# Three stages of an eight-stage transformer kernel: attention with dense experts in two parts over all 32 batches, ReLU experts and a ternary feed-forward without their loops

## The reference, cut to what matters

```python
# stage E (L1_ffn): 16 heads of 8, 8 experts, 2 chosen for each row
q, k, v = split(x @ W_qkv + b_qkv)
attn_out = softmax(q @ k.T / sqrt(8)) @ v
gate = softmax(x @ W_gate + b_gate);  combine = gate kept at its two largest
out = attn_out + sum_e combine[e] * (x @ W_experts[e] + b_experts[e])
# stage G (L2_ffn): 8 experts 128 -> 512 -> 128, mask = 1 at the two largest gates
out = sum_e mask[e] * (relu(x @ w1[e] + b1[e]) @ w2[e] + b2[e])
# stage I (L3_ffn): weights rounded to -1, 0, 1
h = layernorm(gelu(x @ W_fc.T), w, b);  out = h @ W_proj.T
```

## Time and profile before

| what | value |
|---|---|
| median of 3 timed runs | 8145.55 us (8137.73 to 8151.84) |
| profiled execution | 8119.01 us, its span 8117.1 us |
| busy PE / PE weight loads / DVE / ACT / POOL | 79% / 59% / 62% / 35% / 10% |
| mean granted PE clock | 0.829 |

### The profile page before, as it was taken

How to read it: one execution, slowest core, us unless ns; L and a number is a source line. 1 busy time by engine, 2 the same in 40 slices (tenths; PEclk the granted TensorE clock), 3 DMA queues, 4 the chain that set the end, 5 groups by cost and what they waited for, 6 DMA issues and landing times. The chain is left out here.

```text
span 8117.1 us, 210088 instructions
## 1 busy us (share of the span) xinstructions
PE 6394.4 (79%) x89378; PEld 4794.1 (59%) x89401; DVE 5039.5 (62%) x17947; ACT 2829.9 (35%) x4816; POOL 831.3 (10%) x803
## 2 busy tenths in 40 slices
PE   4444589989866698988978868888888888888875
PEld 3333467766643388888856645556556555565653
DVE  6777855455456666666643367577575775756742
ACT  2121133333322311111111135555455554555541
POOL 1114400000000100000000011111110111101100
PEclk7667799999988855555579989999999999999986
DMA  1000000000000000000000000000000000000000
GB/s 31 1 2 1 27 1 1 1 1 1 1 4 0 3 4 4 4 4 4 4 22 0 0 18 2 7 6 2 10 2 4 8 2 10 2 2 10 2 4 10
DMA packets 61243, 45.06 MB, mean 6 GB/s; under 512 B 22521, under 2 KB 56125, under 8 KB 60227
## 3 DMA queue, kind: packets, MB, share of 16 engines
q1 hardware_dynamic: 60355, 32.26, 1.5%
HBM read 30.14 MB, written 2.10 MB: 4 GB/s over the span
## 5 line engine op out<-in xcount | busy, mean ns | idle before, releaser
L368 DVE TENSOR_REDUCE peak<-ps 128x8 f32<-128x1024 f32 (+1 forms) x832 | 816.8, 1023 | 267.1 <-PE ps L290 266.3
L410 ACT ACTIVATE e<-ps,H_lowT_c 77x1024 f32<-77x1024 f32 x384 | 405.6, 1105 | 259.9 <-PE ps L314 259.9
L410 ACT ACTIVATE e<-ps,H_lowT_s 128x1024 f32<-128x1024 f32 x384 | 407.0, 1111 | 248.5 <-PE ps L314 248.5
L328 PEld LDWEIGHTS ps<-e,H_vt 128*32 128x32 f32 (+1 forms) x12288 | 319.8, 112 | 255.5 <-ACT e L410 140.9
L328 PE MATMUL ps<-e,H_vt 128*32 128x128 f32 (+1 forms) x12288 | 432.9, 281 | 23.6 <-DVE xs L388 17.7
L314 PE MATMUL ps<-H_qr,H_km 32*128 32x128 f32 (+1 forms) x12288 | 424.6, 277 | 0.0
L314 PEld LDWEIGHTS ps<-H_qr,H_km 32*128 32x128 f32 (+1 forms) x12288 | 410.2, 170 | 15.4 <-issue 2.2
L1838 PE MATMUL ps<-F_hp,F_encW 128*128 128x1 bf16 (+2 forms) x12288 | 363.4, 166 | 24.7 <-issue 22.4
L1868 PE MATMUL ps<-F_eT,F_ctxp 77*128 77x1 f16 (+1 forms) x12288 | 375.4, 165 | 1.7
L418 ACT ACTIVATE oT<-ps 128x512 f32<-128x512 f32 x416 | 248.4, 597 | 365.9 <-PE ps L328 365.9
L2216 POOL TENSOR_TENSOR H_rstd<-H_veps,neghalf 128x4 f32<-128x4 f32 (+1 forms) x146 | 160.8, 1101 | 2076.3 <-DVE H_veps L2212 2076.3
(11 more groups left out here) (602 smaller groups left out, 14394.4 us busy)
## 6 DMA issues: line engine op xcount, KB each, us to landing
G_w<-in_L_ffn_w SPq DMA_DIRECT2D x16, 256.0 KB
H_f<-in_L_xcond_f_w SPq DMA_DIRECT2D x12, 256.0 KB
H_nw<-in_L_xcond_n_w SPq DMA_DIRECT2D x21, 128.0 KB, 2.1
A_cond<-in_cond SPq DMA_DIRECT2D x1, 2048.0 KB
out_x<-x_all SPq DMA_DIRECT2D x1, 2048.0 KB, 8.7
ctx_rows<-in_ctx SPq DMA_DIRECT2D x1, 1232.0 KB
D_wq<-in_L_xcond_attn_wq SPq DMA_DIRECT2D x2, 512.0 KB
D_wk<-in_L_xcond_attn_wk SPq DMA_DIRECT2D x2, 512.0 KB
```

Source lines behind the costliest of these rows:

```text
L328: last = nc.tensor.matmul(ps[PAD_COLS * s:PAD_COLS * (s + 1), FLAT, r * S:(r + 1) * S], vt_of(u)[0:keys, QUAD * r + s, :], e[0:keys, half, ...
L368: last = nc.vector.tensor_reduce(peak[:, HL * half:HL * (half + 1)], view, AX.X, ALU.max, negate=True)
L410: nc.scalar.activation(e[0:keys, half, :], ps[0:keys, AGAIN[half]:AGAIN[half] + 2, :].rearrange("p b t -> p (b t)"), ACT.Exp, bias=low(u) ...
```

## The change

All three hardware loops are gone; the eight groups are written out in one block each, with counting semaphores in place of the barrier.

In **E** the work is split. The first part takes projections, gates and experts for all 8 groups; queries, keys and value rows of all 32 batches are kept (`qr`, `kr`, `vr`). An expert is now one job over the 4 batches of a group, in one of 4 banks, and DVE adds it at once into `x_all` with 4 scalar-tensor-tensor instructions; the wide multiply, the sum over experts and the tile `moe` are gone. The next group's transposes, projections and logits stand between jobs, at places that `TURN_AT` to `PICK_AT` name. The second part is one attention of 32 units, with the key masks made by ACT within it, values spread by POOL, and the sum into `x_all` after every fourth unit. The statistics of all 32 batches are taken in the preparation. In **G** and **I** the next group's layer norm, transposes and gates move between the experts (G) or beside the hidden layer (I) of the present one; the first group's statistics move to the preparation.

```diff
-km = sb("E_km", [D, QUAD, U * S], scope=st)
-o8 = sb("E_o8", [S, U, D], scope=st)
-moe = sb("E_moe", [S, U, D], scope=st)
+nT = sb("E_nT", [D, 2, U * S], scope=st)
+qr = sb("E_qr", [D, B * S], scope=st)
+kr = sb("E_kr", [D, B * S], scope=st)
+vr = sb("E_vr", [S, B, D], scope=st)
+km = sb("E_km", [D, 2, QUAD, U * S], scope=st)
...
-with nc.Fori(0, NG) as g:
-    with nc.Block() as block:
+with nc.Block() as block:
+    LOGITS, QUERY, KEY, VALUE = 4, 5, 6, 7
+    TURN_AT, QUERY_AT, KEY_AT, VALUE_AT, GATE_AT = 0, 1, 2, 3, 4
+    NORMAL_AT, CENTRE_AT, PICK_AT = 4, 6, 7
+    JOBS = NG * EXPERTS
...
+        def turn(g):
+            pe.wait_ge(sem["z_ready"], g + 1)
+            if g:
+                pe.wait_ge(sem["cand_ready"], g)
+            for u in range(U):
+                last = nc.tensor.transpose(ps[:, LOGITS, u * S:(u + 1) * S], zn[:, u, 0:D], ident[:])
+            last.then_inc(sem["zT_done"], 1)
...
+        turn(0)
+        query(0)
+        logits(0)
+        key(0)
+        value(0)
+        for g in range(NG):
+            for x in range(EXPERTS):
+                j = EXPERTS * g + x
+                if j >= 4:
+                    pe.wait_ge(sem["expert_ready"], j - 3)
+                lay_bias(per(j % 4), for_each(be[:, x * D:(x + 1) * D]))
+                for u in range(U):
+                    last = nc.tensor.matmul(per(j % 4)[:, u, :], nT[:, g % 2, u * S:(u + 1) * S], we[:, x * D:(x + 1) * D], start=False,
+                                            stop=(u == U - 1), skip_group_check=True)
                 last.then_inc(sem["expert_done"], 1)
...
+                if g + 1 < NG:
+                    if x == TURN_AT:
+                        turn(g + 1)
+                    if x == QUERY_AT:
+                        query(g + 1)
+                    if x == KEY_AT:
+                        key(g + 1)
+                    if x == VALUE_AT:
+                        value(g + 1)
+                    if x == GATE_AT:
+                        logits(g + 1)
...
+        def ready(u):
+            g = u // U
+            if u == 0:
+                pe.wait_ge(sem["expert_ready"], JOBS)
...
+                pe.wait_ge(sem["masked_v"], 2)
+            if u % U == 0:
+                pe.wait_ge(sem["masked_a"], QUAD * g + 2)
...
+        small_tensor(pe, 0, B, S, lambda u: qr[:, u * S:(u + 1) * S],
+                     lambda u: km[:, (u // U) % 2, :, (u % U) * S:(u % U + 1) * S],
+                     lambda u: vt[:, (u // U) % 2, u % U], None, ready, ready_values)
...
+        def during(u, part):
+            if part == 1 and u % U < 2 and u + U < B:
+                mask(u // U + 1, 2 * (u % U))
+                mask(u // U + 1, 2 * (u % U) + 1)
+        take(0)
+        take_query(0)
+        gate_exponentials(0)
+        take_key(0)
+        take_rows(0)
+        for g in range(1, NG):
+            take(g)
+            take_query(g)
+            take_key(g)
+            take_rows(g)
+            gate_exponentials(g)
+            if g == 2:
+                mask(0, 2)
+                mask(0, 3)
+        small_scalar(act, 0, B, S, None, during)
...
+        def during(u):
+            if u % U == 2 and u > U:
+                g = u // U - 1
+                dve.wait_ge(sem["o_normed"], U * g + U)
+                xg = x_all[:, g * U:(g + 1) * U, :]
+                step(nc.vector.tensor_tensor(xg, xg, o8[:], ALU.add))
+        normalise(0)
+        normalise(1)
+        centre_gates(0)
+        pick(0)
+        for g in range(NG):
+            for x in range(EXPERTS):
+                j = EXPERTS * g + x
+                dve.wait_ge(sem["expert_done"], j + 1)
+                for u in range(U):
+                    row = x_all[:, g * U + u, :]
+                    last = nc.vector.scalar_tensor_tensor(out=row, in0=per(j % 4)[:, u, :], scalar=picked[:, g % 2, u, x:x + 1],
+                                                          in1=row, op0=ALU.mult, op1=ALU.add)
+                last.then_inc(sem["expert_ready"], 1)
+                dve.wait_ge(sem["expert_ready"], j + 1)
+                if x == NORMAL_AT and g + 2 < NG:
+                    normalise(g + 2)
+                if x == CENTRE_AT and g + 1 < NG:
+                    centre_gates(g + 1)
+                if x == PICK_AT and g + 1 < NG:
+                    pick(g + 1)
+                if x == NORMAL_AT and g + 1 == NG:
+                    mask_first()
+        small_vector(dve, step, 0, B, S, lambda u: o8[:, u % U, :], during)
+        dve.wait_ge(sem["o_normed"], B)
...
+    TURN_AT, GATE_AT, PICK_AT = 4, 5, 6
+    pairs = [(g, x) for g in range(NG) for x in range(EXPERTS)]
...
+        turn_rows(pe, 0, bank=TURN)
+        logits(0)
+        hidden(0)
+        for m, (g, x) in enumerate(pairs):
+            if x == TURN_AT and g + 1 < NG:
+                pe.wait_ge(sem["gate_ready"], g + 1)
+                turn_rows(pe, g + 1, bank=TURN)
+            if m + 1 < len(pairs):
+                hidden(m + 1)
+            if x == GATE_AT and g + 1 < NG:
+                logits(g + 1)
+            jobs_read(pe, 4 * m + 4)
+            if m >= 2:
+                pe.wait_ge(sem["mix_added"], m - 1)
+            lay_bias(per(OUT + m % 2), for_each(b2[:, x * D:(x + 1) * D]))
+            for u in range(U):
                 for c in range(4):
...
+        normalise(0)
+        centre_gates(0)
+        pick(0)
+        relu_job(dve, 0, 1)
+        relu_job(dve, 0, 3)
+        for m, (g, x) in enumerate(pairs):
+            relu_job(dve, m + 1, 1)
+            relu_job(dve, m + 1, 3)
+            ahead = g + 1 < NG
+            if x == 0 and ahead:
+                measure(g + 1)
+            if x == 1 and ahead:
+                normalise(g + 1)
+            dve.wait_ge(sem["mix_done"], m + 1)
+            for u in range(U):
+                row = x_all[:, g * U + u, :]
+                last = nc.vector.scalar_tensor_tensor(out=row, in0=per(OUT + m % 2)[:, u, :], scalar=picked[:, g % 2, u, x:x + 1],
+                                                      in1=row, op0=ALU.mult, op1=ALU.add)
+            last.then_inc(sem["mix_added"], 1)
+            dve.wait_ge(sem["mix_added"], m + 1)
+            if x == GATE_AT and ahead:
+                centre_gates(g + 1)
+            if x == PICK_AT and ahead:
+                pick(g + 1)
...
+        def narrow(g):
+            pe.wait_ge(sem["hidden_scaled"], g + 1)
             for c in range(4):
+                k = 4 * g + c
+                if k >= 2:
+                    pe.wait_ge(sem["pT_ready"], k - 1)
                 for u in range(U):
...
+                    last = nc.tensor.transpose(ps[:, TURN + c % 2, u * S:(u + 1) * S], hid[:, g % 2, u, c * D:(c + 1) * D], ident[:])
                 last.then_inc(sem["turned"], 1)
...
+            pe.wait_ge(sem["pT_ready"], 4 * g + 4)
+            if g:
+                pe.wait_ge(sem["mix_added"], g)
             for u in range(U):
                 for c in range(4):
...
+                    last = nc.tensor.matmul(per(ROWS_OUT)[:, u, :], hidT[:, c, u * S:(u + 1) * S], wpj[:, c * D:(c + 1) * D],
                                             start=(c == 0), stop=(c == 3))
             last.then_inc(sem["mix_done"], 1)
 
...
+        turn_rows(pe, 0, bank=HOLD)
+        for g in range(NG):
+            widen(g)
+            if g + 1 < NG:
+                turn_rows(pe, g + 1, bank=HOLD)
+            if g:
+                narrow(g - 1)
+        narrow(NG - 1)
...
+        take(0)
+        for g in range(NG):
+            gelu(g)
+            if g + 1 < NG:
+                take(g + 1)
+            if g:
+                scale(g - 1)
+        scale(NG - 1)
...
+        def normalise_hidden(g):
+            h = hid[:, g % 2]
+            dve.wait_ge(sem["hid_ready"], U * (g + 1))
+            measure(lambda u: h[:, u, :], stats_h, mv_h, veps_h, "lengths_ready")
+            dve.wait_ge(sem["lengths_inverted"], g + 1)
+            for u in range(U):
+                last = nc.vector.tensor_scalar(h[:, u, :], h[:, u, :], mv_h[:, u, 0:1], rstd_h[:, u:u + 1], ALU.subtract, ALU.mult)
+            last.then_inc(sem["hidden_scaled"], 1)
+        def add(g):
+            dve.wait_ge(sem["mix_done"], g + 1)
+            xg = x_all[:, g * U:(g + 1) * U, :]
+            nc.vector.tensor_tensor(xg, xg, per(ROWS_OUT), ALU.add).then_inc(sem["mix_added"], 1)
+        normalise(0)
+        for g in range(NG):
+            if g + 1 < NG:
+                measure(lambda u: rows(g + 1, u), stats, mv, veps, "var_ready")
+                normalise(g + 1)
+            normalise_hidden(g)
+            if g:
+                add(g - 1)
+        add(NG - 1)```

Three places show the new order. First, PE at the start of a turn of E before (`xnT` is the group's transposed rows, `E_be` the experts' bias; after these rows come seven more pairs of bias and expert, then the attention's L290):

```order
L144 MATMUL ps<-ident,zn 128x128 x4
L1570 MATMUL ps<-xnT,E_wqkv 128x512 x2
```

## The result

| | median of the runs | ratio to before, 95% |
|---|---|---|
| before, measured again beside it | 8141.64 us (8119.64 to 8151.84) | |
| changed kernel | 7752.95 us (7732.77 to 7761.14) | 0.9519 (0.9500 to 0.9539) |

The change saves 388.7 us, 4.8%. The profiled execution of the changed kernel took 7749.24 us (span 7747.5), at a mean granted PE clock of 0.842.

What follows compares the result with a forecast made beforehand. The prediction took PE to bound G, and waits to bound E and I, which no engine fills. Its terms, -165 (E) - 81 (G) - 109 (I) = -355 us, took 8145.6 to 7790 us, range 7750 to 7840.

Steps and rivals of the forecast that it cites:

- E, forecast -165: Stage E: split into two parts plus a longer preparation, it takes 295.6 us against 460.2, saving 165 us.
- Preparation: Stage E: statistics of 32 batches and clearing 4096 columns make DVE free 6.9 us later.
- First part: Stage E: 10.5 us before the first job can be added, then eight groups of 13.2 us, together 116 us.
- Second part: Stage E's attention: 32 units in one pipeline, 169.5 us, plus 1 for masks and sums and 0.7 for the last sum.
- Rival 1: Stage E: the first part does not mesh, 17 us a group; 61 us come back, 7851 us in total; chance 0.15.
- G, forecast -81: Stage G: PE sets the pace at 57.8 us a group, 483.5 us in sum against 564.5, saving 81 us.
- Rival 3: Stage G: PE is held up by gates or layer norm between ReLUs; up to 35 us back, 7825 us; chance 0.07.
- I, forecast -109: Stage I: overlapped rounds of 16.0 us, with the narrow product at low clock, give 135 us against 243.5, saving 109 us.
- transposes did not bring the clock up: Stage I: the narrow product took 5.88 us against 3.57 at high clock, though 3.68 us of transposes came directly before it.
- Rival 2: Stage I: the clock stays high, a round is 13.1 us and I 20 us less; 7770 us in total; chance 0.12.
- Rival 5: All three stages: a wait joins the groups again and nothing overlaps; some 50 us saved, 8095 us; chance 0.01.
- rival 4: The three written-out stages: instruction supply becomes the bound, slower than before, 8295 us at 40 ns per instruction; chance 0.01.

Runs made afterwards that it cites:

- unrolled kernel: The kernel before with its three hardware loops written out eight times, barriers kept and nothing overlapped: 8127.98 us, ratio 0.998.
- better preparation: Changed kernel with G's bias rows waiting only for the three small loads and POOL clearing E's value tile instead of DVE: 7729.62 us; repeated, 7735.27 us.

## Why the prediction was right, and where it was off

**E, forecast -165, measured -165.1.** *Preparation*, +6.9: the first row of the loop came 20.0 us into the stage (2318.84) and comes 27.1 us into it now (2329.91): +7.1. *First part*, 10.5 + 8 x 13.2 = 116: from 2329.91 to the attention's first product at 2446.35 are 116.4 us. Two slips of about 1 us cancel in it, which is luck: the first expert could be added after 11.9 us (2341.82), not 10.5, and the rest took 104.5 us, not 105.6, with groups of 12.90 to 13.47 once the first was through. The prices of PE in the walk are in the trace of before, at 1.00: eight passes of 512 columns 3.44 us (4222.07 to 4225.51), a bias 0.21 (to 4225.72), 16 products of 128 columns 3.57 (to 4229.29). So a bias and 4 products are 1.1 us, and in the changed E one such job is 1.10 (2350.16 to 2351.26). PE and DVE are nearly equal in it, but their waits don't decide: from 2366.0 to 2432.0 PE is hardly ever idle, and DVE waits 0.32 us in most groups, 0.73 in one. *Second part*, 169.5 + 1 + 0.7: from 2446.35 to the end of the last sum, 2617.20, are 170.9. The masks on ACT and the sums on DVE went into existing waits, as costed. Rival 1 did not occur. The two-bank kernel shows what stood behind it: with less room between the engines a group is 14.9 us, so even that reached only half way to the 17 that rival 1 named.

**G, forecast -81, measured -82.8.** PE is the bound, an expert every 7.22 us, and no work inserted on DVE reaches it: from 3984.0 to 4440.0 it is busy for all 456.00 us, at 1.00. From the first scaling to the next stage are 4446.5 - 3964.75 = 481.8 us, forecast 483.5. Rival 3 did not occur.

**I, forecast -109, measured -134.5.** The mechanism was right: wide product, Gelu and hidden layer norm lie beside the narrow chain. The size was not. The step that failed is the sentence "transposes did not bring the clock up", and with it the round of 16.0 us. A round is 12.46 us. The chain itself is the one that the prediction walked; in the second overlapped round its links, from DVE's statistics at 7657.14 on, are 3.77 us to the transposes of the next rows (forecast 3.75), 0.50 for these (1.1), 3.71 for the hidden transposes and scaling (4.55), 3.88 for the narrow product until its sum (5.9) and 0.60 for the sum (0.75). Nearly all of the 3.6 us that are missing from 16.0 lie in PE's three links. They ran at 1.00, where those of before had 0.50 (both groups of transposes) and a mean of 0.63 (narrow product). Rival 2, "the clock stays high in I", is what happened. It had a chance of 0.12, and its price was a round of 13.1 us; the rounds are another 0.6 shorter than that, mostly because at the high clock transposes and scaling take 3.71 us up to the narrow product (7661.41, L2963, to 7665.12) where the sum had kept 4.55.

What was misread is the earlier trace rows. There 16 transposes followed an idle 6.85 us, ran at 0.50 (7973.21 to 7977.00), and the narrow product behind them began at 0.50 (7977.76 to 7980.00). Both are true. But the transposes were only 3.68 us of work, with an idle 0.87 us behind them, and in the changed kernel's first round the clock rose to 0.96 behind transposes without such a gap (4.24 us busy of 4.30), with no product since 7641.53. In three other profiles the same first round did not bring it up in time (last section). Whether the gap, the shorter work or the moment at which it came kept it down in the earlier trace rows was not tried. The row showed that these transposes, after that idle time, had not yet raised the clock. It didn't show that transposes never do, and still less what was needed: that they can't *hold* a clock that is already up. In I after the change the clock is up when they begin. The two kernels with fewer and more transposes show that they hold it.

So the assumption behind -109, that in I transposes leave PE's clock as idle time does, had this one row for it, and three measurements speak against it. In the rows a transpose is one record and an fp32 product two (x16 for 16 of the one, x32 for 16 of the other in the earlier trace rows), so the trace does tell them apart. But for the fp32 transposes of this kernel the clock went from 0.50 to 0.96 after 4.24 us of transposes alone, stayed at 1.00 over 7.90 us in which PE did nothing else, and was 0.50 when the narrow product began with twelve of sixteen taken out. By the assumption the first could not happen, and the other two would have left PE equally idle, with the clock falling in both.

**The sum.** -355 forecast, -382.4 measured by stages, of which 25.5 is I, 1.8 G and 0.1 E. The medians differ by 388.7. The median of before fell from 8145.6 to 8141.6 in the later runs, and the untouched stages add or take some ten us in any one execution. That the time lies in the range is in part luck. The prediction's own sum with small slips (7760 to 7815, chance 0.64) missed it; the range reached lower because of rival 2 ("the high clock in I") and "a run like the profiled one", and it held by 3 us. Rival 5 (only barriers saved) is refuted by the periods above, rival 4 (instruction supply) by the unrolled kernel (504.87 us of PE in G for 505.40).

## What to carry to other kernels

When two stages of work are laid side by side, walk one period for each engine with durations from the trace. Here it gave the period within 0.3 us in E and in G. For PE ask as well what the overlap does to its clock. In I the narrow product took 3.84 us instead of 5.88 once the idle time around it had shrunk, and the high clock in I was worth more than the error of all other terms together (25.5 us against 1.9). One row that agrees with an assumption is no test of it: look for a row in which the assumption and its opposite would differ, and if there is none, keep both prices with chances nearer to each other than 0.64 to 0.12. Judge a term of one per cent by its stage in the trace, not by the median of the kernel.

## What the hardware showed beyond that

The clock in I is not the same in every execution with the same order of work. In the changed kernel it rose before the first narrow product (3.84 us at 7652.66), and so it did in the repeated better preparation. In three other profiles (only I changed, two banks in E, the better preparation for the first time) the same transposes after the same idle 5.61 us ran at 0.50 as well, but the clock rose only within the narrow product behind them (0.50 in its first 1.7 us, a mean of 0.72 to 0.77 in the rest), which took 5.54, 5.62 and 5.42 us. Timeline of the kernel with only I changed:

```profile
7924.28 5.54 PE L2768 MATMUL ps<-I_wpj,I_hidT 128*128 128x128 f32 x32 [0.87 <-ACT I_hidT L2795]
```

In these three the first wide product, too, was slower (6.62, 6.77 and 6.36 us for 5.12, at 0.53 to 0.56 for 0.70). Together these are at least 2.8 of the 3.4 to 3.6 us by which their stage I is longer (123.5 to 123.7 for 120.1 in the table): clock again, not order. What decides between the two is open. So that all sixteen transposes *hold* a clock that is up was seen in every round but one (below); that they *raise* it, only in some profiles.

The changed kernel kept 1.00 from 7652.6 on. The version with the layer norm further ahead lost it once in mid-stage (the row of 5.47 us above). That fall cost 1.6 us (5.47 for 3.84). What starts it isn't settled.

Stage H, the same code in all twelve profiles, took 3153.6 to 3202.0 us. Its windows in the shortest (layer norm further ahead) and the longest (unrolled) of them, columns as above:

```profile
4432.20:7585.83 3153.63, 2636.44 (x38088) 1810.08 (x38088) 2131.97 (x5443) 1682.37 (x2580) 439.90 (x434) 0.95 0.02 6
```

```profile
4705.90:7907.90 3202.00, 2695.54 (x38088) 1850.98 (x38088) 2128.99 (x5433) 1684.21 (x2580) 440.33 (x434) 0.93 0.02 6
```

The same 38088 matmul records take PE 59 us more at a mean clock of 0.93 than at 0.95, while DVE, ACT and POOL take the same within 3 us. In the other ten profiles, too, the two go up together (3165.7 us with 2651.34 of PE, 3189.2 with 2680.85). So most of the spread of this kernel's times is the spread of PE's granted clock in its longest stage. No experiment here was aimed at what decides it.
